# A mixture-of-experts decoder layer in which expert results are added to the output by accumulating indirect transfers

## The reference, cut to what matters

```python
x = x + attn(layernorm(x))                       # linear attention, 16 heads
x = x + xattn(layernorm(x), ctx)                 # cross attention with 4 groups, alibi
def ffn(x):                                      # x: 2048 tokens of 256; 8 experts, 2 per token
    probs = softmax(x @ gate_w.T)
    weights, indices = top_k(probs, 2)
    weights = weights / weights.sum(-1)
    for each token t and its experts e:          # H = 176
        out[t] += weights[t, e] * (silu(x[t] @ w_gate[e]) * (x[t] @ w_up[e])) @ w_down[e]
    sh = silu(x @ shw_gate) * (x @ shw_up) @ shw_down
    return out + sigmoid(x @ shgate_w) * sh
x = x + ffn(layernorm(x))
```

## Time and profile before

| | us |
|---|---|
| median of 3 runs | 484.37 |
| lowest, highest | 481.43, 485.26 |
| span of the profiled execution, first to last instruction | 481.2 |

### The profile page before, as it was taken

How to read it: one execution, slowest core, us unless ns; L and a number is a source line. 1 busy time by engine, 2 the same in 40 slices (tenths; PEclk the granted TensorE clock), 3 DMA queues, 4 the chain that set the end, 5 groups by cost and what they waited for, 6 DMA issues and landing times.

```text
span 481.2 us, 12458 instructions
## 1 busy us (share of the span) xinstructions
PE 389.4 (81%) x4000; PEld 326.6 (68%) x4000; DVE 298.3 (62%) x809; ACT 230.6 (48%) x576; POOL 215.6 (45%) x252
## 2 busy tenths in 40 slices
PE   6787889888898898998987878199999999999400
PEld 4466667666676676776866668189998888889300
DVE  1455777778777777778653297146765665556265
ACT  1233466544665446644653476057635555555200
POOL 1134376665766657665463004735403334343300
PEclk9698999999999989989999989679999999999755
DMA  8720105141041510500000001211213333333286
GB/s 243 198 97 12 53 5 143 54 140 58 5 137 53 140 53 0 140 11 12 12 2 1 2 0 49 105 67 66 81 51 101 111 118 108 106 111 111 75 283 220
DMA packets 30422, 40.13 MB, mean 83 GB/s; under 512 B 6322, under 2 KB 23602, under 8 KB 30386
## 3 DMA queue, kind: packets, MB, share of 16 engines
q1 hardware_dynamic: 24626, 28.09, 20.4%
q0 software_dynamic: 3456, 9.46, 5.5%
q10 hardware_dynamic: 2304, 2.10, 1.3%
HBM read 22.82 MB, written 16.81 MB: 82 GB/s over the span
## 4 chain that ended last, share of the span: by engine, by line
PE 57%; DVE 17%; issue 12%; DMA 5%; ACT 3%; another core or an unknown queue 2%; POOL 2%; DVEq 1%; POOLq 0%; ACTq 0%; SPq 0%
PE ps L749 17%; PE ps L523 6%; PE ps L640 4%; PE ps L587 3%; PE ps L627 3%; DMA yg<-y_rows 3%; DVE sc L1227 3%; PE ps L530 3%; PE ps L602 3%; PE ps L568 2%; DMA y_rows<-e_y,out_row 2%; PE ps L593 2%; DVE xn L1221 2%; PE ps L679 2%
## 5 line engine op out<-in xcount | busy, mean ns | idle before, releaser
L497 POOL DMA_INDIRECT y_rows<-e_y,out_row x40 | 38.5, 962 | 69.7 <-ACT e_y L1093 33.6
L749 PE MATMUL ps<-w_hi,xh 128*128 (+1 forms) x144 | 50.8, 353 | 17.0 <-DVE xl L1346 14.3
L438 POOL TENSOR_TENSOR sc<-sc,smax 128x1024 f32<-128x1024 f32 x16 | 31.7, 1984 | 43.4 <-DVE smax L1233 43.4
L489 POOL DMA_INDIRECT xs_rows<-x_send,pos x32 | 31.0, 969 | 40.3 <-DVE pos L1445 19.7
L749 PE MATMUL ps<-w_hi,xl 128*128 (+1 forms) x144 | 47.8, 332 | 0.0
L749 PE MATMUL ps<-w_lo,xh 128*128 (+1 forms) x144 | 47.5, 330 | 0.0
L749 PEld LDWEIGHTS ps<-w_hi,xh 128*128 128x128 f32 x144 | 27.8, 193 | 21.5 <-issue 14.2
L431 POOL TENSOR_TENSOR bias_t<-alibi,key_off 128x1024 f32<-128x1024 f32 x16 | 37.9, 2368 | 0.0
L404 POOL TENSOR_TENSOR st<-mv,eps 128x1 f32<-128x1 f32 x32 | 6.1, 192 | 65.7 <-DVE mv L1147 33.8
L523 PE MATMUL ps<-wkv,xn1T 128*128 128x512 f32 x64 | 32.8, 638 | 0.5 <-ACT xn1T L929 0.5
L1221 DVE TENSOR_SCALAR xn<-x_all,mv,rs 128x256 f32<-128x256 f32 (+1 forms) x16 | 28.6, 1789 | 2.1 <-POOL rs L406 1.9
(11 more groups left out here) (179 smaller groups left out, 1178.0 us busy)
## 6 DMA issues: line engine op xcount, KB each, us to landing
w_stage<-in_w_ffn_dram SPq DMA_DIRECT2D x12, 496.0 KB, 3.9
xs_rows<-zeros SPq DMA_DIRECT2D x5, 1028.0 KB, 7.7
xs<-xs_rows SPq DMA_DIRECT2D x40, 128.5 KB
yg<-y_rows SPq DMA_DIRECT2D x16, 256.0 KB, 3.9
ctx_sb<-in_ctx_dram SPq DMA_DIRECT2D x16, 128.0 KB, 2.0
out_dram<-y ACTq DMA_DIRECT2D x16, 128.0 KB, 4.0
x_all<-in_x_dram SPq DMA_DIRECT2D x1, 1792.0 KB, 10.3
y_rows<-e_y,out_row POOLq DMA_INDIRECT x40
```

The source lines that it names most:

```text
L438: nc.gpsimd.tensor_tensor(v, v, spread(smax[:, :].rearrange("p (h o) -> p h o", o=1), 2, S), ALU.subtract).then_inc(sm["sub_ready"], 1)
L489: nc.gpsimd.indirect_dma_start(out=xs_d[:, :], out_offset=bass.IndirectOffsetOnAxis(ap=pos[:, t, r:r + 1], axis=0), in_=x_send[:, t, r, :] ...
L497: nc.gpsimd.indirect_dma_start(out=y_d[:, :], out_offset=bass.IndirectOffsetOnAxis(ap=out_row[:, q:q + 1], axis=0), in_=e_y[:, q, :], in_o ...
L749: mm = T.matmul(out_ap, lhs, rhs[rows, cols], start=st, stop=en)
```

## The change

- The output tensor in HBM gets 512 dump rows ahead of the 2048 real ones (cut off again on return); they are zeroed at the start.
- A row sent to an expert has two extra elements: the output row of its token (the same for both experts of a token), and half the token's weight for this expert. DVE uses the latter as the scalar of e_h, in place of the constant 0.5, so that the down product comes out weighted. `load_slots` waits for e_h of tile i-4 as well.
- Stage 4 is gone. Each x3 tile is stored to the output by SP as soon as it is made: tiles 0 to 13 ahead of the first load of a slot tile, tiles 14 and 15 between the fourth and the fifth.
- POOL adds `e_y` to the output rows with an indirect transfer that accumulates (`add_out`), after all 16 stores. Two tiles of one expert hold different tokens, so their adds may overlap; tiles of different experts may share a token. DVE makes a table `turn_i` (16 where a tile's expert differs from the one before, else 0). Add i waits for adds i-3 to i-1 to have landed if its turn is 16 (adds 0 to 4 always; adds 5 and 6 always for those of tiles 2 and 3), and otherwise only for the earlier use of their buffers. From tile 5 on POOL reads the turn into a register. Its loop over groups of four is written out.
- 39 slot tiles instead of 40 (the sum over experts can't exceed 39); four of them hold no token here, against five before.

The diff, cut to its core (the sizes of `x_send`, `xs` and `zeros` become `ROW`, and loops over slot tiles end at 39 on each engine):

```diff
-SLOT_TILES = 2 * TILES + NE
-SPARE = SLOT_TILES * P
+ROW_TILES = 2 * TILES + NE
+SLOT_TILES = ROW_TILES - 1
+ROW = D + 2
+DUMP = 4 * P
...
-        yg = sb("yg", [P, 4, 2, D])
-        y1 = sb("y1", [P, 2, D])
-        y2 = sb("y2", [P, 4, D])
-
-
-
-        xs_d = nc.dram_tensor("xs_rows", (SLOT_TILES * P, D + 1), F32).ap()
-        y_d = nc.dram_tensor("y_rows", (SPARE + 2 * B * S, D), F32).ap()
+        xs_d = nc.dram_tensor("xs_rows", (ROW_TILES * P, ROW), F32).ap()
...
+            sp.dma_start(out_d[0:DUMP, :].rearrange("(n p) d -> p n d", p=P),
+                         spread(zeros[:, 0:D].rearrange("p (o d) -> p o d", o=1), 1, 4)).then_inc(sm["dump_zeroed"], 16)
...
                 wait(sp, sm["out_row_ready"], i - 3)
+                wait(sp, sm["e_h_ready"], i - 3)
                 sp.dma_start(xs[:, q, :], xs_d[bass.ds(i * P, P), :]).then_inc(sm[f"xs_in{q}"], 16)
 
+            def store_x3(t):
+                sp.wait_ge(sm["x3_ready"], t + 1)
+                sp.dma_start(out_d[DUMP + t * P:DUMP + (t + 1) * P, :], x_all[:, t, :]).then_inc(sm["x3_stored"], 16)
+
+            for t in range(TILES - 2):
+                store_x3(t)
             sp.wait_ge(sm["sent"], 2 * 16 * TILES)
             for i in range(4):
                 load_slots(i, i)
+            for t in range(TILES - 2, TILES):
+                store_x3(t)
             with sp.Fori(1, SLOT_TILES // 4) as quad:
                 i = 4 * quad
                 for q in range(4):
                     load_slots(i + q, q)
-
-            def load_y(t, q):
-                wait(sp, sm["y_ready"], t - 3)
-                sp.dma_start(yg[:, q, :, :], y_d[bass.ds(t * 2 * P + SPARE, 2 * P), :].rearrange("(p r) d -> p r d", r=2)
-                             ).then_inc(sm[f"y_in{q}"], 16)
-
+            for i in range(SLOT_TILES // 4 * 4, SLOT_TILES):
+                load_slots(i, i % 4)
             for q in range(4):
-                sp.wait_ge(sm[f"ys_out{q}"], 4 * SLOT_TILES)
-            for t in range(4):
-                load_y(t, t)
-            with sp.Fori(1, TILES // 4) as quad:
-                t = 4 * quad
-                for q in range(4):
-                    load_y(t + q, q)
-            for q in range(4):
-                sp.wait_ge(sm[f"stored{q}"], 4 * TILES)
+                sp.wait_ge(sm[f"added{q}"], 16 * len(range(q, SLOT_TILES, 4)))
+            sp.wait_ge(sm["x3_stored"], 16 * TILES)
+            sp.wait_ge(sm["dump_zeroed"], 16)
...
+            pool.wait_ge(sm["weights_ready"], 1)
...
-            def scatter_out(i, q):
+            def add_out(i, q):
+
+
                 pool.wait_ge(sm["out_row_ready"], i + 1)
                 pool.wait_ge(sm["e_y_ready"], i + 1)
+                turned = pool.value_load(turn_i[0:1, i:i + 1], min_val=0, max_val=16) if i > 4 else 16
+                for j in range(max(i - 3, 0), i):
+                    before = j // 4
+                    pool.wait_ge(sm[f"added{j % 4}"], 16 * before + (turned if before else 16))
                 alone(pool, sm["pool_passed"])
                 nc.gpsimd.indirect_dma_start(
-                    out=y_d[:, :], out_offset=bass.IndirectOffsetOnAxis(ap=out_row[:, q:q + 1], axis=0),
-                    in_=e_y[:, q, :], in_offset=None).then_inc(sm[f"ys_out{q}"], 16)
-
-            for i in range(4):
-                scatter_out(i, i)
-            with pool.Fori(1, SLOT_TILES // 4) as quad:
-                i = 4 * quad
-                for q in range(4):
-                    scatter_out(i + q, q)
+                    out=out_d[:, :], out_offset=bass.IndirectOffsetOnAxis(ap=out_row[:, q:q + 1], axis=0),
+                    in_=e_y[:, q, :], in_offset=None, compute_op=ALU.add).then_inc(sm[f"added{q}"], 16)
+
+            pool.wait_ge(sm["turns_ready"], 1)
+            pool.wait_ge(sm["dump_zeroed"], 16)
+            pool.wait_ge(sm["x3_stored"], 16 * TILES)
+            for i in range(SLOT_TILES):
+                add_out(i, i % 4)
...
-                wait(act, sm[f"ys_out{q}"], 4 * (i - q))
+                wait(act, sm[f"added{q}"], 4 * (i - q))
...
-            def store_out(t, q):
-                act.wait_ge(sm["y_ready"], t + 1)
-                act.dma_start(out_d[bass.ds(t * P, P), :], y2[:, q, :]).then_inc(sm[f"stored{q}"], 16)
...
+            V.tensor_scalar(x_send[:, :, :, D + 1:D + 2].rearrange("p t r o -> p t (r o)"),
+                            w_choice[:, :, :].rearrange("p r t -> p t r"), 0.5, None, ALU.mult).then_inc(sm["weights_ready"], 1)
...
+                chained(V.tensor_tensor(turn[:, 1:], slot_e[:, 1:], slot_e[:, 0:SLOT_TILES - 1], ALU.not_equal))
+                V.tensor_scalar(turn_i[:, 1:], turn[:, 1:], 16.0, None, ALU.mult).then_inc(sm["turns_ready"], 1)
...
-                V.scalar_tensor_tensor(out=e_h[:, p, :], in0=e_gg[:, p, :], scalar=0.5, in1=ps[:, EG + p, H:2 * H],
+                V.scalar_tensor_tensor(out=e_h[:, p, :], in0=e_gg[:, p, :], scalar=xs[:, q, D + 1:D + 2], in1=ps[:, EG + p, H:2 * H],
...
-                wait(v, sm[f"ys_out{q}"], 4 * (i - q))
-                V.tensor_tensor(out_row[:, q:q + 1], xs[:, q, D:D + 1], spare_rows[:, bass.ds(i, 1)], ALU.max
+                wait(v, sm[f"added{q}"], 4 * (i - q))
+                V.tensor_tensor(out_row[:, q:q + 1], xs[:, q, D:D + 1], dump_row[:, q:q + 1], ALU.max
...
-            def combine(t, q):
-                p = q % 2
-                v.wait_ge(sm[f"y_in{q}"], 4 * (t - q) + 16)
-                V.scalar_tensor_tensor(out=y1[:, p, :], in0=yg[:, q, 0, :], scalar=w_choice[:, 0, bass.ds(t, 1)], in1=xt(t),
-                                       op0=ALU.mult, op1=ALU.add).then_inc(sm["y1_ready"], 1)
-                v.wait_ge(sm["y1_ready"], t + 1)
-                wait(v, sm[f"stored{q}"], 4 * (t - q))
-                V.scalar_tensor_tensor(out=y2[:, q, :], in0=yg[:, q, 1, :], scalar=w_choice[:, 1, bass.ds(t, 1)], in1=y1[:, p, :],
-                                       op0=ALU.mult, op1=ALU.add).then_inc(sm["y_ready"], 1)
-
-            for t in range(4):
-                combine(t, t)
-            with v.Fori(1, TILES // 4) as quad:
-                t = 4 * quad
-                for q in range(4):
-                    combine(t + q, q)
+            for i in range(SLOT_TILES // 4 * 4, SLOT_TILES):
...
-        "out_rows": (2 * (np.arange(TILES)[None, :, None] * P + pos[:, None, None]) + np.arange(2) + SPARE).astype(np.float32),
-        "spare_rows": (np.arange(SLOT_TILES)[None, :] * P + pos[:, None]).astype(np.float32),
+        "out_rows": (DUMP + np.arange(TILES)[None, :, None] * P + pos[:, None, None] + np.zeros(2)).astype(np.float32),
+        "dump_row": (pos[:, None] + P * np.arange(4)).astype(np.float32),
```

More of the change, by code:

```diff
@@ L48 @@
 WARM_UP = 10
-ZERO_TILES = SLOT_TILES // (W_PARTS // 2 - 1)
+ZERO_TILES = ROW_TILES // (W_PARTS // 2 - 1)
 W_PART = -(-W_END // (2 * W_PARTS)) * 2
@@ L122, in build @@
         ones_b = sb("ones_b", [P, P], BF16)
-        zeros = sb("zeros", [P, D + 1])
+        zeros = sb("zeros", [P, ROW])
         w_hi = sb("w_hi", [P, W_ALL], F32R)
@@ L167, in build @@
         slot_ei = sb("slot_ei", [1, SLOT_TILES], I32)
+        turn = sb("turn", [1, SLOT_TILES])
+        turn_i = sb("turn_i", [1, SLOT_TILES], I32)
         sgt = sb("sgt", [P, TILES])
@@ L240, in build @@
         s_hl = sb("s_hl", [P, 2, 3, P], F32R)
-        xs = sb("xs", [P, 4, D + 1])
+        xs = sb("xs", [P, 4, ROW])
         out_row = sb("out_row", [P, 4], U32)
@@ L273, in build @@
             ln3_st ln3_mv neg_mean_ready ln3_ve ln3_rs ln3_nb ln3_done xT_mm xn3T_ready route_mm logits_ready
-            routing lgs_ready pe8_ready sgt_ready sg4_ready hotb_ready rank_mm pos_ready slots_ready sent
+            routing lgs_ready pe8_ready sgt_ready sg4_ready hotb_ready rank_mm pos_ready slots_ready turns_ready weights_ready sent
             s_x_ready rows_ready s_xT_mm s_xh_ready s_xl_ready s_gate_mm s_up_mm
@@ L285, in build @@
         ctx_d = a["ctx"].rearrange("b s d -> (b s) d")
-        out_d = out.rearrange("b s d -> (b s) d")
+        out_d = out
         def bcast(vec, n):
@@ L1109, in _ @@
                 experts(i, i % 4, i >= 1, i >= 2, True)
-            with act.Fori(2, SLOT_TILES // 4 - 1) as quad:
+            with act.Fori(2, SLOT_TILES // 4) as quad:
                 i = 4 * quad
@@ L1113, in _ @@
                     experts(i + q, q, True, True, True)
-            for q in range(4):
-                experts(SLOT_TILES - 4 + q, q, True, True, q < 2)
-            h_high(SLOT_TILES - 1, 1)
-            copy_y(SLOT_TILES - 2, 2)
-            copy_y(SLOT_TILES - 1, 3)
-            def store_out(t, q):
-                act.wait_ge(sm["y_ready"], t + 1)
-                act.dma_start(out_d[bass.ds(t * P, P), :], y2[:, q, :]).then_inc(sm[f"stored{q}"], 16)
-            with act.Fori(0, TILES // 4) as quad:
-                t = 4 * quad
-                for q in range(4):
-                    store_out(t + q, q)
+            for i in range(SLOT_TILES // 4 * 4, SLOT_TILES):
```

(33 more changed lines are left out.)

11 lines of the change are left out of this document (5 added, 6 removed).

## The result

| | before | after |
|---|---|---|
| median, us | 482.9 (481.1 to 485.3, 4 runs) | 509.96 (508.55 to 511.34, 4 runs) |
| span of the profiled execution, us | 481.2 | 509.5 |

The ratio is 1.0548, 95% interval 1.0505 to 1.0591: 5.5% slower. The prediction, 488.1 us with a range up to 504, was wrong. The profiled execution is the one of 511.34 us. Each ratio here leaves out a run that lies more than 1.5% above the fastest of its kernel (one of the kernel before, one of the last variant of the changed kernel). The page of the changed kernel answers to the earlier trace rows and, for q0, to the earlier trace rows; then its row of the adds, of out_row, and of the transfers' landing.

A forecast was written before the change was run, and what follows sets the result against it. It took a four-buffer ring (2.25 us a tile, over PE's 2.11) to bound the expert stage. First add at 367.0 + 110.6 + 7.4 = span 485.0, +3.8 on 481.2; added to the median, 488.1 us, range 470 to 504.

The forecast's parts named there:

- a ring of four buffers: Expert stage: scatter(i) to out_row(i+4), then out_row to scatter, closes over four tiles: 9.0 us, 2.25 a tile, before the change.
- R: Expert stage: one turn of the four-tile ring, 6.65 + L' = 10.7 us, with the expert turns at tiles 12, 16, 20 hidden.
- L': Expert stage: from an add's start to out_row four tiles later, 4.05 us; each microsecond of it worth 13.
- the ring, not PE's 2.11, is already last: Expert stage of the kernel before: the buffer ring at 2.25 us a tile sets the pace, above PE's 2.11.
- The prediction's own formula: Expert stage, first to last add: 7S + 6R + 14.1 = 13 L' + 57.9 = 110.6 us.
- the price of the add: Accumulating transfer in the expert stage: +1.2 us over the plain scatter, taken between bounds of +0 and +2.0.
- S: Expert stage: step of an add that waits for the one before to land, L' + 0.55 = 4.6 us.
- rival 2: Accumulating add in the expert stage costs only a second pass, +0.37 us: span 474.2, time 477.4; chance 0.28.
- Rival 1: Accumulating add in the expert stage costs a full read more, +2.0 us: span 495.4, time 498.5; chance 0.25.
- Rival 3: Expert stage: the buffer ring does not bind and the stage stays as it is: about 466 us; chance 0.05.
- the register load: POOL reads each add's turn from tile 5 on: 0.5 us more between out_row and the add.
- the start of the stage: First slot-tile loads stand behind x3 stores on SP: 3.2 + 1.4 = 4.6 us, first add at 367.0.

The follow-up runs named there:

- last variant of the changed kernel: Changed kernel with out_row(i) moved to the end of DVE's work for tile i, buffers and waits kept: 494.87 us, ratio 1.0204.
- last experiment: Kernel before with out_row(i) moved to the end of DVE's work for tile i: 484.31 us beside 482.88, ratio 1.0018.
- second profile of the changed kernel: Changed kernel run again unaltered, on a chip with the shorter times: 492.45 us beside 466.67 for the kernel before, ratio 1.0547.
- second group: Runs on three chips where the kernel before takes 466.7 to 468.6 us, not 482.9, and PE is busy 13.00 of 13 us from 300 to 313 us.
- kernel before with 40 columns: Kernel before with 40 columns of out_row, so DVE doesn't wait for the scatter of tile i-4, and POOL's loop written out: 461.15 us, ratio 0.9872.

## Why the prediction was wrong, point by point

- **The step that failed** is the reading of the ring: "This is a ring of four buffers", with out_row(i) until scatter(i) as its leg, and from it "Tiles 12, 16, 20 follow at R each, their turns hidden" and "Each microsecond of L' is worth 13". The prediction itself listed the two tiles of PE work between out_row and the scatter, but not that the down products of the tile *before* stand in the same program behind h of this one. In the trace of before, out_row(9) at 377.69 was followed 3.59 us later by scatter 8:

```profile
381.28 0.96 POOL L497 DMA_INDIRECT y_rows<-e_y,out_row  x1 [1.78 <-ACT e_y L1093]
```

- That loop is 3.59 + 2.85 = 6.44 us for three tiles, 2.15 a tile: close under the 2.32 of the stage, so it was easy to miss. With the longer add it is 8.35, and a turn, which must wait for the last of the three to land, comes on top. 38 steps at 12.96 for four are 123.1 us. The estimate is rough, since the first four steps took 19.0 us and tiles 17 to 22 hold no turn; but a walk from add to add with 4.65 us at the start and at turns, at least 8.35 from each add to the third after it, and else 1.85, comes to 123.5, or to 120.7 without the ring at the last add.
- **A reading that the runs leave in doubt** is "the ring, not PE's 2.11, is already last" in the kernel before: with the wait behind the tile's own work (last experiment) it was not faster.
- **The 20.2 us, divided.** The prediction's own formula with measured sizes gives 111.9, so the sizes were off by 1.3. The structure gives 123.1 - 111.9 = 11.2. The other 7.7 (both by that estimate) lie in turns longer than 12.96 us. Those are not the ones in which the clock is low. These are the windows of the turns that end with adds 12, 16, 20 and 32; the clock is the third number from the end:

```profile
403.83:416.79 12.96, 10.54 (x65) 9.79 (x65) 6.02 (x22) 5.25 (x17) 6.20 (x4) 0.87 0.52 83
416.79:430.65 13.86, 10.21 (x72) 9.22 (x71) 6.30 (x23) 5.75 (x18) 6.20 (x5) 1.00 0.45 78
430.65:443.83 13.18, 10.74 (x59) 10.05 (x58) 4.95 (x17) 4.84 (x14) 6.21 (x4) 0.74 0.51 80
471.11:486.07 14.96, 10.62 (x64) 9.72 (x64) 6.04 (x22) 5.33 (x16) 6.20 (x4) 0.89 0.44 72
...
406.02 0.32 PE L752 MATMUL ps<-w_hi,xl 128*128 x1
...
411.08 0.49 PE L752 MATMUL ps<-w_hi,xl 128*128 x1
```

- The turn of 12.96 us had a clock of 0.87, and slow matmuls in it (0.49 us in place of 0.32, at 411.08); one of 13.86 had 1.00. The second profile of the changed kernel has the same pair, 13.00 at 0.87 and 13.80 at 1.00. What is longer in the turn at 1.00 is the step to add 16, 5.61 us in place of 4.61: the landing of add 15 was seen 4.40 us after its start, that of add 11 after 3.74, and POOL took 1.21 us from there to the add in place of 0.87. Add 16 comes 5.60 us after add 15 in the second profile too, and at add 32 the step is 5.63 and 5.24. Why those landings are late stays open, and so do the 7.7 us. Low clock may cost something elsewhere; no run shows how much.
- **Right: the price of the add.** +1.2 predicted, +1.1 measured; L' is 4.13 us on average (4.03 in the second profile) against 4.05; S 4.6 predicted, 4.71 to 4.85 measured at adds 1 to 4 (4.63 to 4.95 in the second). The second pass alone (rival 2, +0.37) is refuted: the packets double as it supposes, but 1.5 us of landing come with them. Rival 1 has the wrong cause, though its time was nearer. Rival 3 is refuted: the stage grew by 40 us. That the price came out right is in part luck, since it was taken between two bounds, with no row of an accumulating transfer.
- **Too small: the register load**, 0.77 for 0.5, once in each ring; taking 0.55 of it away gave 7.4 us.
- **Too small: the start of the stage**, 4.6 for 8.65 (in the second group 6.0: 353.80 beside 347.77 in the kernel before with 40 columns). The chain of the changed kernel shows why (start, us):

```profile
353.99 0.34 DVE x_all L1379
354.35 0.33 SPq L372
354.72 2.50 DMA xs<-xs_rows
357.35 1.19 PE ps L832 x4
...
365.61 0.34 SPq L372
...
366.39 2.10 DMA xs<-xs_rows
```

- Both stands are where they were predicted: behind the store of tile 13, and behind that of tile 15. But x3 of tile 13 is 1.4 us later (353.99 + 0.34, against 352.94), the load took 2.50 us in place of 2.0, and after the stand PE ran at a granted clock of 0.66 from 354 to 364 us, where it had 1.00 in the kernel before. x3 of tile 15 was then 6.8 us late instead of 3.2.
- **Right: the end**, 7.66 for 7.4. The last add lands under POOL's drain. The term for e_h in load_slots was rightly put at nothing: PE waited 5.0 us in two places for slot tiles, both at the start. No run tests DVE's routing by itself.
- **The range** took its upper end from the price of the add, with a coefficient of 13. The walk above has 19 steps that grow with L', so the same bounds would have lain wider apart, and higher. The doubt belonged to the shape of the ring, and none was put there.

## What to carry to other kernels

A ring is not read off the number of its buffers: follow the late release through every in-order program, and look which *older* tile's work stands behind the instruction that it frees. Here a wait of a tiny address computation held a ring of four at three tiles, and giving that operation its own columns cost 140 bytes a partition and gave back 25 us. When a transfer gets longer, ask first which waits for it can be removed or moved behind the tile's own work, before its price is multiplied by the number of tiles.
